# Attention in a two-layer graph network: query and key products of four graphs in one 512-column matmul, and VectorE's softmax scales ahead of the residual sum

## The reference, cut to what matters

```python
q, k, v = split_heads(x @ Wq.T), split_heads(x @ Wk.T), split_heads(x @ Wv.T)
bias = (adj + adj)[:, None]
a = einsum('bhnd,bhmd->bhnm', q, k) * 512 ** -0.5 + bias
a = where(any(a != 0, axis=-1, keepdims=True), a, -inf)
p = softmax(a, axis=-1)                      # a row of nan becomes 0
o = einsum('bhnm,bhmd->bhnd', p, v)          # heads joined again: [128, 128, 512]
x = layernorm(x + o @ Wo.T)                  # x1, goes to layer 1
```

## Time and profile before

| | us |
|---|---|
| median of three runs (2769.44 to 2771.19) | 2769.57 |
| the profiled execution's own time | 2769.48 |
| its span, first to last instruction | 2767.7 |
| attention | from 0 to about 2000 |
| experts | about 2000 to 2510 |
| final normalisation | about 2510 to the end |

### The profile page before, as it was taken

One profiled execution on the slowest core, in us unless ns is written; L12 is line 12 of the kernel. 1 busy time (PEld: TensorE's weight loads), 2 busy tenths in 40 slices (PEclk: granted clock), 3 DMA queues, 4 the chain that ended last, 5 costly groups with the idle time before them and its releaser, 6 DMA issues. The chain is left out here.

```text
span 2767.7 us, 78092 instructions
## 1 busy us (share of the span) xinstructions
PE 2675.1 (97%) x22706; PEld 2277.7 (82%) x22707; DVE 1922.3 (69%) x8351; ACT 1514.3 (55%) x5391; POOL 1282.3 (46%) x1174
## 2 busy tenths in 40 slices
PE   8999999999999999999999999999899999998776
PEld 7898989898989898989888888888788888885232
DVE  6777777777777777777777777777733333335887
ACT  5565656565666666565656565656534444442444
POOL 2334333333434343434333333343356666666887
PEclk9999999999999999999999999999999999999999
DMA  4111111111111111111111111111234444445999
GB/s 147 63 53 54 53 62 53 54 53 62 53 54 53 62 53 54 53 62 53 54 55 60 57 50 58 57 58 49 78 121 136 133 135 135 138 135 199 397 406 349
DMA packets 169428, 277.33 MB, mean 100 GB/s; under 512 B 19378, under 2 KB 52146, under 8 KB 168882
## 3 DMA queue, kind: packets, MB, share of 16 engines
q1 hardware_dynamic: 150962, 243.36, 26.3%
q10 hardware_dynamic: 18432, 33.56, 3.2%
HBM read 184.57 MB, written 92.27 MB: 100 GB/s over the span
## 5 line engine op out<-in xcount | busy, mean ns | idle before, releaser
L564 POOL TENSOR_TENSOR kept<-kept,row_scale 128x512 f32<-128x512 f32 x512 | 533.5, 1042 | 1107.7 <-DVE row_scale L448 1097.9
L342 ACT ACTIVATE kept<-kept,neg_max 128x128 f32<-128x128 f32 x2048 | 795.9, 397 | 138.5 <-DVE neg_max L424 138.5
L424 DVE CUSTOM_DVE_ANT_0 kept<-att_bank,adj_nat 128x128 f32<-128x128 f32 x2048 | 442.6, 286 | 3.5 <-PE att_bank L212 1.6
L342 ACT ACTIVATION_READ_ACCUMULATOR kept<-kept,neg_max 128x1 f32 x2048 | 401.2, 196 | 0.0
L433 DVE TENSOR_REDUCE abs_max<-kept 128x4 f32<-128x512 f32 x512 | 349.2, 682 | 0.1
L191 PE MATMUL att_bank<-xt_hi,w_hi 128*128 128x256 f32 x2048 | 329.8, 284 | 11.0 <-DVE w_lo L401 11.0
L191 PE MATMUL att_bank<-xt_hi,w_lo 128*128 128x256 f32 x2048 | 330.1, 284 | 0.0
L191 PE MATMUL att_bank<-xt_lo,w_hi 128*128 128x256 f32 x2048 | 329.5, 283 | 0.0
L191 PEld LDWEIGHTS att_bank<-xt_hi,w_hi 128*128 128x128 f32 x2048 | 299.3, 191 | 30.5 <-issue 10.6
L375 ACT ACTIVATE kept<-att_bank 128x512 f32<-128x512 f32 x256 | 153.2, 599 | 278.8 <-PE att_bank L255 278.7
L191 PEld LDWEIGHTS att_bank<-xt_hi,w_lo 128*128 128x128 f32 x2048 | 283.2, 192 | 0.0
(11 more groups left out here) (142 smaller groups left out, 5267.8 us busy)
## 6 DMA issues: line engine op xcount, KB each, us to landing
kept<-in_x_t SPq DMA_DIRECT2D x64, 512.0 KB, 3.4
kept<-in_x SPq DMA_DIRECT2D x128, 256.0 KB, 2.6
x_scratch<-kept SPq DMA_DIRECT2D x128, 256.0 KB, 2.0
g_x<-x_scratch SPq DMA_DIRECT2D x128, 256.0 KB, 2.8
n_x<-x_scratch SPq DMA_DIRECT2D x128, 256.0 KB, 7.2
out_x<-n_x ACTq DMA_DIRECT2D x128, 256.0 KB, 5.5
y_scratch<-g_out SPq DMA_DIRECT2D x96, 256.0 KB, 2.0
n_y<-y_scratch SPq DMA_DIRECT2D x96, 256.0 KB, 5.7
```

The lines of the kernel that those rows point to most:

```text
L342: nc.scalar.activation(probs[:, h * P:(h + 1) * P], neg_s[:, h * P:(h + 1) * P], ACT.Exp, bias=neg_max[:, h:h + 1], scale=-1.0, accum_out= ...
L424: nc.vector.tensor_tensor_reduce(neg_s[:, h * P:(h + 1) * P], bank[r][:, c * P:(c + 1) * P], adj_nat[:, s], -2.0, BIG, ALU.add, ALU.min, n ...
L564: nc.gpsimd.tensor_tensor(part, part, by, ALU.mult).then_inc(probs_done, 1)
```

## The change

GROUP goes from 2 to 4: x comes transposed for four graphs, and a unit is 12 matmuls of 512 columns (a whole PSUM bank). Two units a step replace four. The loop takes eight steps a turn, 15 turns, with the last eight written out. Ahead of the loop the first group of four is made in two halves, 16 units of 256 columns and not 8, followed by two full units; in the last eight steps the remaining units of the last group come again as halves, with 2, 2, 2, 3, 3, 0, 0, 0 of them in the steps. Query and key of alternate groups live in tiles that the later phases use (`g_x1` with half of `w_stage`, and `out_sum` with `out_sq`). Because of that the weights of values and output are loaded at once into other tiles, and the expert weights are loaded near the end of attention. `adj_nat` and five small tiles move into the last two slots of `kept`, so that the profile will name them `kept`. VectorE does all four quarters of `largest`, `inverse`, `scales` and only then the residual sum, its statistics and its own unit copy. The transposed x is cut once in four steps, in two halves.

```diff
-GROUP = 2
+GROUP = 4
...
+    TAIL = 2 * UNROLL
...
+    TAIL_UNITS = [(n, 0) for n in range(UNITS, 2 * C)] + [(n, 1) for n in range(UNITS, 2 * C)]
+    TAIL_COUNTS = (2, 2, 2, 3, 3, 0, 0, 0)
...
+    def units_of_step(t, s, g, last):
+        if not last:
+            first = (s + 1) % UNROLL * UNITS
+            par = (g + 1 + (s + 1) // UNROLL) % 2
+            return [(HEAD_UNITS + UNITS * t + k, first + k, None, par) for k in range(UNITS)]
...
-        qk = [half[:, :, :].rearrange("p (w a) (b n) -> p w (a b) n", w=2, n=GN) for half in pair]
+        adj_nat = kept[:, 30].rearrange("p (u n) -> p u n", u=UNROLL)
+        qk = [(g_x1, w_stage[:, 0]), pair]
+        staged = [w_stage[:, 0], w_stage[:, 1], x1, kept[:, 2 * C:3 * C]]
...
-            with eng.Fori(0, LAST // UNROLL) as i:
+            with eng.Fori(0, LAST // TAIL) as i:
...
             def body(t, s, i, ...):                                        # SyncE
-                if s % 2 == 0 and not last:
-                    g = i * 2 + s // 2
-                    sp.wait_ge(xt_lo_done, g + 1)
-                    load_xt(g + 2, s // 2)
+                if s == 0 and not last:
+                    sp.wait_ge(xt_lo_done, i * 2 + 4)
+                    load_xt(i + 2)
...
             def body(t, s, i, g, last):                                    # TensorE
...
-                    qk_unit(AHEAD + 4 * t + k, k, ahead % 2, (ahead // 2) % 2, BANK_B - k % 2)
+                    qk_unit(u, half, par, BANK_B - place)
...
             def body(t, s, i, g, last):                                    # VectorE
                 copy_pt(t, 2)
-                if s % 2 and not last:
-                    dve.wait_ge(v_ps, t + 1)
-                    dve.wait_ge(xt_in[s // 2], i * 16 + 32)
-                    nc.vector.tensor_copy(xt_hi[:, s // 2], xt_stage[:, s // 2]).then_inc(xt_hi_done, 1)
+                if s == 2 and not last:
+                    dve.wait_ge(v_ps, t + 2)
+                    dve.sem_inc(xt_turn, 1)
+                    dve.wait_ge(xt_in, i * 16 + 32)
+                    for half in range(2):
+                        cut_xt(g, half)
...
                     largest(t + 1, 1)
+                    inverse(t + 1, 1)
+                    scales(t + 1, 1)
+                    largest(t + 1, 2)
+                here = [(unit, k) for k, unit in enumerate(units_of_step(t, s, g, last)) if place_of(t, k, last) == 1]
...
+                if more:
+                    inverse(t + 1, 2)
+                    scales(t + 1, 2)
+                    largest(t + 1, 3)
+                    inverse(t + 1, 3)
+                    scales(t + 1, 3)
                 dve.wait_ge(wo_ps, t + 1)
                 dve.wait_ge(x_in[s], i * 16 + 16)
                 nc.vector.tensor_tensor(res[:, s % 2], bank[BANK_WO][:, :], x_nat[:, s],
                                         ALU.add).then_inc(res_done, 1)
-                if more:
-                    inverse(t + 1, 1)
-                    scales(t + 1, 1)
...
```

More of the change, by code:

```diff
@@ L172, in body @@
                 if last and t == B - 2:
[L173 to L178, removed]
+                    load_expert_w(2, e_lo_done, 1)
+                if last and t == B - 6:
+                    load_expert_w(0, s_ps, B - 4)
+                    load_expert_w(1, w_lo_done, 2)
+                if last and t == B - UNROLL:
+                    for n in range(UNROLL):
+                        sp.wait_ge(x1_out[n], 32)
+                        sp.dma_start(g_x1[:, n], x1_dram[n]).then_inc(g_x1_in[n], 16)
+                        sp.dma_start(adj_t[:, n, 0:P], io["adj_t"][n]).then_inc(g_adj_in[n], 16)
             for_steps(sp, body)
@@ L204, in v_parts, with scores @@
                     yield
-            def scores(s):
-                par, j = (s // 2) % 2, s % 2
+            def scores(par, j):
                 for c in range(C):
@@ L320, in body @@
                 mm.then_inc(wo_ps, 1)
-                if more_units:
-                    for k in range(1, UNITS):
-                        next_unit(k)
+                for k, unit in enumerate(units[1:], 1):
+                    next_unit(*unit, place_of(t, k, last))
             for_steps(pe, body)
@@ L367, in _, with body @@
             exps(0, range(12, HEADS))
[L368 to L372, removed]
+            for n in range(2 * C, 4 * C, 2):
+                copy_qk(n, n - 2 * C, 1, 0)
+                if n == 3 * C - 2:
+                    cut_w(O)
+            copy_qk(4 * C, 0, None, 1)
+            def body(t, s, i, g, last):
                 for c in (1, 3):
@@ L379, in body @@
                                      ACT.Copy).then_inc(o_hi_done, 1)
-                ahead = s + 3
+                here = [(unit, k) for k, unit in enumerate(units_of_step(t, s, g, last)) if place_of(t, k, last) == 0]
                 if exists(t, last, 1):
@@ L384, in body @@
                     copy_v(t + 2, (s + 2) % UNROLL, BANK_WO)
-                for k, heads in ((0, range(3, 9)), (2, range(9, HEADS))):
+                for late, heads in ((False, range(3, 9)), (True, range(9, HEADS))):
                     if exists(t, last, 1):
                         exps(t + 1, heads)
-                    if exists(t, last, 3):
-                        copy_qk(AHEAD + 4 * t + k, k, ahead % 2, (ahead // 2) % 2)
+                    for unit, k in here:
+                        if late == (k > 0):
+                            copy_qk(*unit)
                 if last and t >= B - 3:
                     e = t - (B - 3)
-                    cut_expert(e, *((qk_ps, 4 * B) if e < V else (v_ps, B)))
+                    cut_expert(e, *((qk_ps, units_so_far(B - 1)) if e < V else (v_ps, B)))
             for_steps(act, body)
@@ L524, in body @@
                 if more:
-                    largest(t + 1, 3)
-                    inverse(t + 1, 3)
-                    scales(t + 1, 3)
-                if more:
                     copy_pt(t + 1, 0)
-                if exists(t, last, 3):
-                    copy_qk(AHEAD + 4 * t + 3, C - 1, ahead % 2, (ahead // 2) % 2)
+                for unit, k in here:
+                    if k > 0:
+                        copy_qk(*unit)
                 dve.wait_ge(rstd_done, t + 1)
@@ L564, in normalise, with body @@
                 nc.gpsimd.tensor_tensor(part, part, by, ALU.mult).then_inc(probs_done, 1)
-            xt_low(0, 0)
-            xt_low(1, 1)
+            for n in range(4):
+                xt_low(n + 1, n // 2, n % 2)
             for c in range(C):
                 normalise(0, c)
-            def body(t, s, i, last):
-                if s % 2 and not last:
-                    xt_low(i * 2 + s // 2 + 2, s // 2)
+            def body(t, s, i, g, last):
+                if s == 2 and not last:
+                    for half in range(2):
+                        xt_low(i * 2 + 5 + half, g, half)
                 if exists(t, last, 1):
```

204 lines of the change are left out of this document (115 added, 89 removed).

## The result

The changed kernel takes 2755.41 us (median of five runs, 2753.68 to 2757.58); the kernel before took 2769.57 in the same comparison. The ratio is 0.9953, with a 95% interval of 0.9943 to 0.9964. It is faster by 14.2 us, 0.5%.

The account below looks back on a forecast made before the run. TensorE, with a matmul in flight for 1930.10 of 1931.00 us, was taken to bound the kernel. From 2769.48, -33.6 (units), +10.0 (ahead of the loop) and -7.3 (last steps) gave 2739 us, range 2729 to 2758.

Parts of the forecast that it names:

- the first rival: Loop return: longer turns no longer fit, so each of 15 returns fetches its first block again; 2743 to 2776 us; chance 0.20.
- the cover of 0.75: VectorE's copy of transposed quarter 2 ends at T+2.99, is needed at T+3.74; T is the start of a step's transposes.
- The price range of 0 to 2.5 us: Cost of one loop return: 0 if the engine has work queued, 2.5 us by the smallest DMA's time to landing.
- The units: Loop: two units of 12 512-column matmuls replace four of 256; 0.28 us less a step, -33.6 us over 120 steps.
- The rival that a wide matmul saves little: Loop units: with a fixed part of 2.5 ns a matmul, 120 steps give only -7.2 us; 2765 us; chance 0.04.
- the sum's own range: Whole kernel: 2730 (-38, +10, -11.5) to 2743 us (-30, +10, -7.3).
- Ahead of the loop: Before the first transposes: 16 half units and two full ones add 11.2 us; step 0 gives back 1.2; +10.0 us.
- The last eight steps: Steps 120 to 124, with 2, 2, 2, 3, 3 units: 69.4 us against 76.7, -7.3 us, -11.5 at most.
- The bound taken, 13.86: Steps 120 to 122: the softmax allows no step under 13.86 us, though TensorE's own sum falls to 12.45.
- TensorE waits for no residual sum: Sign of a right forecast in the new trace: VectorE's residual sum never holds up TensorE.
- The covers: Slack in a loop step: about 0.65 us for the residual sum, 0.75 for quarter 2's copy, 0.44 for ScalarE's unit copy.
- the rival of the late residual sum: VectorE's residual sum: scales over 0.65 us late make TensorE wait before every transposes; 2805 us at 1.2 slip; chance 0.08.

Follow-up runs that it names:

- Two kernels that take this cost away: The changed kernel with VectorE's first 120 steps written out (2737.65 us), or with VectorE's loop begun elsewhere in the step, its return inside a wait (2737.52 us).

## Why the prediction was right or wrong

**The step that failed is the return of the loop.** The sum gave it no term, and the first rival, with a chance of 0.20, had it. The sum went by a trace in which turns half as long ran without fetching, and put the longer ones at nothing too. It came as that rival said: packets all through the loop and a longer step at every eighth. Its price on VectorE lay within the rival's bounds too: 1.75 us less the cover of 0.75 makes 1.0, which is TensorE's wait (14.1 in 14). Over the loop, with what follows, it is 1821.39 - 1804.84 = 16.6 us. Two kernels that take this cost away measure 2737.5 and 2737.7. The forecast of 2739 plus 16.6 is 2755.6; that this meets the measured 2755.4 so closely is luck, since 1.3 us missed ahead of the loop and 1.5 in the last steps are cancelled by 0.8 in the loop and by 1.7 behind attention, a part that lies between 808.8 and 812.5 us in these profiles.

The working had weighed TensorE most, at up to 37.5 us, and there the return cost about 1 us in all. 12 wide matmuls stand ahead of it, and the kernels with moved returns show that the place of a return decides; that it is the work ahead of it fits the packets of two of them, and the third ran into a large load. The rival spoke of this ("0 if the engine still has work in its queue") without asking which engine has it. The last instruction of VectorE's turn takes 0.54 us. The price range of 0 to 2.5 us, taken from a DMA's time to landing, is about right on VectorE (1.75 and 2.5 on average), and not on TensorE, where a badly placed return idled it for 5.2 and lowered the clock.

**The units were right.** 15.03 a step against 15.05; with narrow units 15.32 comes back in the regular steps. The rival that a wide matmul saves little falls.

**Two slips in the sums** change nothing: 15 turns have 14 returns within the loop, and the upper end of the sum's own range, -30 + 10 - 7.3, is 2742 and not 2743.

**Ahead of the loop**: +12.5 against +11.2, and step 0 lost its 1.2 us as forecast (15.03 against 16.52). The first matmul starts 2.0 later (13.02 against 10.99), so the new work itself is 10.5.

**The last eight steps**: -5.8 against -7.3. The bound taken, 13.86, came from a step in the old order, with the residual sum ahead of the scales. At the start of steps 121 to 123 TensorE waits for the residual sum, which the new order puts behind all scales, so here the sign "TensorE waits for no residual sum" failed:

```profile
1872.26 1.91 PE L292 MATMUL att_bank<-ident,kept 128*128 128x128 f32 x16
1886.34 1.97 PE L292 MATMUL att_bank<-ident,kept 128*128 128x128 f32 x16 [1.47 <-DVE kept L566]
1900.51 1.97 PE L292 MATMUL att_bank<-ident,kept 128*128 128x128 f32 x16 [1.49 <-DVE kept L566]
```

**The covers held in the loop.** The residual sum was forecast to end at T+14.4. In the step from 156.08 to 171.11 it starts at

```profile
169.69 0.69 DVE L566 TENSOR_TENSOR kept<-att_bank,kept 128x512 f32<-128x512 f32 x1
```

and ends at T+14.3, 0.7 ahead of the transposes. VectorE's copy of quarter 2 was forecast to end at T+2.99 and ends at T+2.98. The copies of units, answering to the earlier trace rows (what, count, busy us, mean ns, idle before), were sized right to 0.02:

```profile
L457 DVE TENSOR_SCALAR out_sum<-att_bank 128x512 f32<-128x512 f32 x29 | 19.7, 680 | 0.0
...
L374 ACT ACTIVATE out_sum<-att_bank 128x512 f32<-128x512 f32 x29 | 16.8, 578 | 0.0
```

In the loop the rival of the late residual sum did not come; 0.7 us a step kept it away.

## What to carry to other kernels

When a change makes a loop's turn longer, ask of each engine whether its turn still runs from what is on the core (packets of instructions in the DMA view tell), what that engine has queued just ahead of the return, and whether a large load is under way at that moment. If the turn no longer fits, put the return where the engine waits anyway: here the same instructions in the same order were 18 us faster. Behind a few long instructions it cost less than behind many short ones (2777 against 2809 us). And an engine that is busy for only 72% of the time can still hold up the one that is busy for all of it.

## What the runs showed of the hardware

- The cost of a return that is fetched again depends on its place. On VectorE it is 1.75 and 2.5 us of idle time on average in two kernels, and nothing inside a 2.0 us wait in a third. On TensorE it is at most 0.5 us of idle time behind 12 matmuls of 512 columns, 1.8 behind 24 of 256, and 5.2 behind 64 of 128 with a load of 1024 KB under way.
- Five kernels have 65 such waits (the changed one, the kernel before with eight steps on VectorE, the narrow units, and the two moved returns of TensorE). In all of them the engine goes on 1.4 to 1.9 us after the last packet on its queue has landed; what differs is when that packet starts, from 2.6 us before the engine runs out of work to 3.1 after.
- VectorE's turn of four steps ran without fetching (one packet in 1800 us), its turn of eight steps did not; the traces count 297 and 583 instructions in such a turn.
- After 5.17 idle us TensorE's granted clock was 0.51 (the 1.2 GHz level) for 6.1 us. In the kernel with narrow units it stayed at 1.00 (2.4 GHz) after 1.83 idle us, and at another return after 2.13 it was 0.50 for 3.3 us, which made that step 16.9 long. It fell at three of the 14 returns, behind 2.04, 2.10 and 2.13 idle us, and stayed up at two others behind 2.10 and 2.12, so the idle time alone does not tell which:

```profile
172.90:175.20 2.30, 0.47 (x5) 0.28 (x3) 0.34 (x3) 0.00 (x0) 0.56 (x1) 1.00 0.39 114
175.20:178.00 2.80, 2.80 (x21) 2.62 (x22) 2.15 (x4) 1.20 (x2) 0.00 (x0) 1.00 0.04 9
```

```profile
548.70:552.00 3.30, 3.26 (x16) 3.26 (x17) 2.11 (x4) 0.60 (x1) 0.00 (x0) 0.50 0.02 5
```
